# Groups 6 and 7 of a fused transformer block: softmax pieces exponentiated in one ScalarE instruction instead of eight

## The chip, the cores and the metric

The kernel runs on one NeuronCore of a Trainium2 chip. Five instruction queues run side by side: TensorE (PE, with its weight loads as PEld), VectorE (DVE), ScalarE (ACT), GpSimd (POOL) and SyncE (SP). Each takes its instructions strictly in the order in which they are written and waits on semaphores where it needs another engine. The metric is the device time of one execution in microseconds; less is better.

## What is computed

Two batches of 1024 tokens of width 256 pass four layers, each added to its input: a 16-head cross attention on 77 context rows, a feed-forward layer of width 1024 with a layer norm behind it, a single-head cross attention on the same context, and a linear layer whose weights are picked by token position. The change touches the softmax of the first layer:

```python
scores = jnp.einsum('bqhd,bkhd->bhqk', q, k) * scale
weights = jax.nn.softmax(scores, axis=-1)
out = jnp.einsum('bqhk,bkhd->bqhd', weights, v).reshape(B, Lq, D)
```

## The kernel before

The 2048 tokens are cut into 8 groups g of 256. A group has two tiles i of 128 tokens, and the 16 heads fall into two halves a of 8 heads. So a group has four score pieces (g, i, a), each 128 tokens by 8 heads x 77 keys = 616 columns. All groups run through all four layers in a software pipeline: while groups 6 and 7 are in the first layer (about 150 to 200 us of the span), groups 3 to 5 are in the feed-forward and the second attention. The order on each engine is a list written out by hand (the calls at the end of `tensor`, `vector`, `scalar` and `gpsimd`). No scheduler changes it.

The steps of a piece in the first layer, in order:

- `sc` (TensorE, L386): the scores, into one of the two score halves of PSUM, S0 or S1.
- `smax` (VectorE, L666): the negated maximum by head. Where `apart(g, i, a)` holds, `smax` also adds it to the 616 columns (L671), which moves them from PSUM to the tile E in SBUF.
- `ex` (ScalarE): where `apart` holds, one exp over 616 columns of E (L1058). Otherwise eight exps of 77 columns, one a head, straight from PSUM with the maximum as bias and the row sum as a second output (L1067).
- `ssum` (VectorE): where `apart` holds, it first sums E by head (L680); then in both cases the reciprocal (L683).
- `en` (GpSimd, L1261): two multiplications of 308 columns by the reciprocals.
- `tE` (TensorE, L396) transposes E into the same score halves, `et` (ScalarE) copies it out, `pv` (TensorE, L408) multiplies by the values, `o` (ScalarE, L1084) copies the result, `wo` (TensorE, L268) is the output projection, and `x1` (VectorE, L688) adds it to the tokens.

A score half is let go by `sub` (the subtraction) where `apart` holds and by `ex` where it does not. The four banks PB0 to PB3 carry everything else of TensorE; each is let go by the step that reads it, and the next piece in the same bank waits for that.

Names of other steps that stand between these: `lo` (L645) takes the low half of a transposed tile for the split multiplication, and `lo("B", 4)` lets go of PB3, in which `cp(2, 3)` (L455, a transpose of the second attention) comes next. `ql` (L653) is the same for the queries and waits for `qh` on ScalarE. `hl` (L693) is the low half of the hidden layer; it is read by `w2`, and `hl(5, 3)` also lets go of the bank that `w2(5, 0, 0)` takes. `y` (L700) takes the feed-forward's result, `x3_` (L738) that of the second attention. On GpSimd, `bo` (L1254) adds a bias and `rs` (L1215 to L1226) makes the scale and shift of a norm from its statistics. On ScalarE `apply` (L1034) normalises, `hh` (L1090) takes the hidden layer out, and `pc` (L1127) copies tokens for the last layer.

Of the kernel before, what the change touches and what calls it, by code (L numbers as in the profile page):

```python
# [63 lines left out]


def apart(g, i, a):
    return a == 1


def apart_upto(n):  # L70

    return sum(apart(m // 4, m % 4 // 2, m % 2) for m in range(n + 1))


def program(nc, A, out):
    with ExitStack() as ctx:
# [177 lines left out]
        def tensor(e):  # L254
# [119 lines left out]
            def sc(g, i, a, k):  # L374
                b, n = g // 4, 4 * g + 2 * i + a
                w.wait_ge(s["ql"], g + 1)
                w.wait_ge(s["qh"], g + 1)
                w.wait_ge(s["kbl"], b + 1)
                w.wait_ge(s["kba"], 4 * b + 4)
                P = hold(("sc", g, i, a), ("S", k), ("sub", apart_upto(n)) if apart(g, i, a) else ("ex", n + 1))  # L380
                ts = slice(i * 128, (i + 1) * 128)

                for j, (Q, KB) in enumerate(((XTH, KBH), (XTH, KBL), (XTL, KBH))):
                    for u in range(2):
                        own = slice(64 * u, 64 * u + 64)
                        t = e.matmul(P[:, u * 512:u * 512 + 4 * NK], Q[own, 1 + g % 2, a, ts],  # L386
                                     KB[own, b, 4 * a:4 * a + 4, :].rearrange("p h k -> p (h k)"),
                                     start=j == 0, stop=j == 2)
                t.then_inc(s["sc"], 1)
# [175 lines left out]
        def vector(e):  # L565
# [92 lines left out]
            def smax(g, i, a):  # L658

                n = 4 * g + 2 * i + a  # L660
                sv = two(bank("sc", g, i, a))[:, :, 0:4 * NK].rearrange("p u (h k) -> p u h k", k=NK)
                w.wait_ge(s["sc"], n + 1)
                if g:
                    w.wait_ge(s["ex"], n - 3)
                top = two(SX[:, i, 0, 8 * a:8 * a + 8])
                e.tensor_reduce(top, sv, AX, ALU.max, negate=True).then_inc(s["mx"], 1)  # L666
                if apart(g, i, a):
                    w.wait_ge(s["mx"], n + 1)
                    if g:
                        w.wait_ge(s["tE"], n - 3)  # L670
                    e.tensor_tensor(E[:, i, a, 0:8 * NK].rearrange("p (u h k) -> p u h k", u=2, h=4), sv,  # L671
                                    top.unsqueeze(3).to_broadcast([128, 2, 4, NK]), ALU.add).then_inc(s["sub"], 1)
# [782 lines left out]
```

## Time and profile before

| | |
|---|---|
| median of three runs | 271.42 us (271.34 to 272.66) |
| the profiled execution | 271.57 us, of it a span of 269.7 us |
| TensorE busy | 247.4 us, 92% |
| VectorE busy | 218.2 us, 81% |
| GpSimd busy | 189.6 us, 70% |
| ScalarE busy | 160.7 us, 60% |

The rows further below come from this one execution. A timeline row gives the start, the duration, the instruction and, in brackets, how long the engine was idle before it and what ended that. Durations of neighbouring instructions overlap by their pipelines, so what an instruction really costs its engine is the distance from its start to the start of the next. TensorE's matmul ends are modelled; the starts of its weight loads show when a step was let in. A row of the same line with "x2" stands for several instructions in a row.

### The profile page before, as it was taken

Reading aid. Unit: us, or ns where it says so; the run is one execution under the profiler, and the core shown is the slowest. Engines: PE = TensorE matmul, PEld = TensorE weight load, DVE = VectorE, ACT = ScalarE, POOL = GpSimd, SP = SyncE. Lnnn points to the kernel's source line nnn. Section 1 sums busy time; section 2 is a strip of 40 time slices with the busy share of each in tenths; the row PEclk is TensorE's granted clock in tenths of the full one; section 3 lists DMA queues with packets and bytes.
Section 4 is the critical chain, followed back from the end, with each engine's and each line's share of the span. In section 5 each row is a group of like instructions: output and inputs, shape, how many; then the busy total and the mean of one; then the engine's idle time right before and its main releaser. Section 6 shows DMA issues by size and latency. Waiting matters only on the chain.

```text
span 269.7 us, 6211 instructions
## 1 busy us (share of the span) xinstructions
PE 247.4 (92%) x2048; PEld 219.3 (81%) x2048; DVE 218.2 (81%) x573; ACT 160.7 (60%) x510; POOL 189.6 (70%) x361
## 2 busy tenths in 40 slices
PE   0977799899799999999999999999999999979990
PEld 0776577599798978999799789998989999967880
DVE  2799998999999798982999977898588776879551
ACT  2449795885364676797375888457566442465530
POOL 3267789897859797867298687988789655615474
PEclk9995999999999999999999999999999999999998
DMA  6993020010201155010001411221071000000033
GB/s 167 319 319 121 0 79 2 2 39 12 70 0 43 39 166 187 5 21 2 0 2 39 101 39 57 63 80 40 2 218 55 2 0 2 0 1 4 0 156 156
DMA packets 11156, 17.61 MB, mean 65 GB/s; under 512 B 1377, under 2 KB 7509, under 8 KB 11125
## 3 DMA queue, kind: packets, MB, share of 16 engines
q1 hardware_dynamic: 9333, 11.98, 14.2%
q0 software_dynamic: 1792, 5.24, 6.6%
q8 instruction: 16, 0.26, 0.4%
q14 instruction: 15, 0.12, 0.2%
HBM read 14.07 MB, written 3.15 MB: 64 GB/s over the span
## 4 chain that ended last, share of the span: by engine, by line
PE 70%; DVE 13%; POOL 5%; issue 4%; ACT 4%; DMA 2%; SPq 0%; POOLq 0%; DVEq 0%
PE PB L275 33%; PE PB L268 13%; PE PB L472 7%; PE PB L348 5%; PE S L396 5%; PE PB L408 4%; PE S L386 4%; ACT E L1067 2%; DVE SX L666 2%; DMA WKV<-in_w_k 2%; POOL E L1261 1%; DVE SX L680 1%; POOL SM L1218 1%; DVE XTL L645 1%; POOL out_x L1314 1%
## 5 line engine op out<-in xcount | busy, mean ns | idle before, releaser
L1261 POOL TENSOR_TENSOR E<-E,SX 128x308 f32<-128x308 f32 x64 | 43.9, 712 | 10.0 <-DVE SX L683 9.8
L1067 ACT ACTIVATE E<-S,SX 128x77 f32<-128x77 f32 x128 | 39.4, 337 | 10.7 <-DVE SX L666 10.7
L275 PE MATMUL PB<-XTH,W1H 128*128 128x256 f32 x128 | 37.3, 291 | 1.6 <-DVE XTL L645 1.4
L275 PE MATMUL PB<-W2H,HH 128*128 128x256 f32 x128 | 37.5, 293 | 0.0
L275 PE MATMUL PB<-W2H,HL 128*128 128x256 f32 x128 | 35.7, 279 | 0.0
L275 PE MATMUL PB<-W2L,HH 128*128 128x256 f32 x128 | 35.7, 279 | 0.0
L275 PE MATMUL PB<-XTL,W1H 128*128 128x256 f32 x128 | 35.6, 278 | 0.0
L275 PE MATMUL PB<-XTH,W1L 128*128 128x256 f32 x128 | 35.5, 278 | 0.0
L1218 POOL TENSOR_TENSOR SM<-SM,nhalf 128x2 f32<-128x2 f32 x40 | 28.4, 711 | 3.1
L1090 ACT ACTIVATE HH<-PB 128x512 fp32r<-128x512 f32 x32 | 19.1, 600 | 15.9 <-PE PB L275 15.6
L1077 ACT ACTIVATE EW<-S 124x640 f32<-124x640 f32 x32 | 21.9, 711 | 10.8 <-PE S L396 10.7
L1067 ACT ACTIVATION_READ_ACCUMULATOR E<-S,SX 128x1 f32 x128 | 28.0, 219 | 0.0
L275 PEld LDWEIGHTS PB<-XTH,W1H 128*128 128x128 f32 x128 | 24.1, 189 | 2.5 <-DVE XTL L645 1.6
L1215 POOL TENSOR_TENSOR SM<-SM,eps 128x2 f32<-128x2 f32 x32 | 6.7, 210 | 27.3 <-DVE SM L625 27.2
L693 DVE SCALAR_TENSOR_TENSOR HL<-PB,HH 128x512 fp32r<-128x512 f32 x32 | 21.1, 677 | 5.5 <-ACT HH L1090 3.4
L622 DVE BATCH_NORM_STATS2 SM<-X 128x6 f32<-128x256 f32 x64 | 23.7, 413 | 1.6 <-DMA X<-in_x 1.4
L666 DVE TENSOR_REDUCE SX<-S 128x8 f32<-128x616 f32 x32 | 24.5, 785 | 0.7 <-PE S L386 0.7
L275 PEld LDWEIGHTS PB<-W2H,HH 128*128 128x128 f32 x128 | 24.1, 188 | 1.1 <-issue 1.0
L1034 ACT ACTIVATE XN<-X,SM 128x256 f32<-128x256 f32 (+1 forms) x32 | 18.9, 601 | 9.9 <-POOL SM L1224 8.3
L396 PE MATMUL S<-ident,E 128*124 128x128 f32 x160 | 22.1, 274 | 2.6 <-POOL E L1261 1.7
L275 PEld LDWEIGHTS PB<-W2L,HH 128*128 128x128 f32 x128 | 24.2, 189 | 0.1
L275 PEld LDWEIGHTS PB<-W2H,HL 128*128 128x128 f32 x128 | 24.1, 189 | 0.0
(203 smaller groups left out, 727.2 us busy)
## 6 DMA issues: line engine op xcount, KB each, us to landing
RAW<-in_w SPq DMA_DIRECT2D x4, 512.0 KB, 6.0
WD<-in_WD SPq DMA_DIRECT2D x8, 256.0 KB, 3.9
X<-in_x SPq DMA_DIRECT2D x4, 256.0 KB, 5.9
x<-X SPq DMA_DIRECT2D x4, 256.0 KB, 2.2
E<-in_WD SPq DMA_DIRECT2D x4, 256.0 KB
bc<-in_rows SPq DMA_DIRECT2D x1, 640.0 KB, 6.2
X<-in_w1r SPq DMA_DIRECT2D x1, 512.0 KB, 7.9
RT<-in_WD SPq DMA_DIRECT2D x2, 256.0 KB, 2.9
```

The source lines that it names most:

```text
L268: t = e.matmul(dst, a, b, start=j == 0, stop=j == len(pairs) - 1)
L275: t = e.matmul(dst, a, b, start=first and j == 0, stop=last and j == n - 1)
L396: t = e.transpose(P[0:CW, c * 128:(c + 1) * 128], E[:, i, a, c * CW:(c + 1) * CW], ident[:, :])
L622: step(e.bn_stats(smi(K, g, i, 0, 6), src[:, i, :]))
L666: e.tensor_reduce(top, sv, AX, ALU.max, negate=True).then_inc(s["mx"], 1)
L693: e.scalar_tensor_tensor(out=HL[:, hs, :], in0=two(bank("w1", g, j)[:, :]), scalar=0.0, in1=f(HH[:, hs, :]), op0=ALU.max, op1=ALU.subtract ...
L1034: e.activation(dst_of(K, g)[:, 1, 0:n], src_of(K, g)[:, 1, 0:n], ACT.Identity, bias=smi(K, g, 1, 10, 11), scale=smi(K, g, 1, 9, 10)).then_ ...
L1067: t = e.activation(Ei[:, h * NK:(h + 1) * NK], P[:, at:at + NK], ACT.Exp, bias=SX[:, i, 0, k:k + 1], accum_out=SX[:, i, 1, k:k + 1])
L1077: e.activation(ET[:, g % 2, a, :, ts], P[0:CW, 0:640].rearrange("p (c t) -> p c t", c=5), ACT.Copy).then_inc(s["et"], 1)
L1090: e.activation(HH[:, 2 * j:2 * j + 2, :], two(bank("w1", g, j)[:, :]), ACT.Relu).then_inc(s["hh"], 1)
L1218: e.tensor_tensor(sm(K, g, 9), sm(K, g, 8), nhalf[:, :], ALU.pow).then_inc(s["rs" + K], 1)
L1261: t = e.tensor_tensor(Eh, Eh, SX[:, i, 2, 8 * a + h:8 * a + h + 4].unsqueeze(2).to_broadcast([128, 4, NK]), ALU.mult)
```

## The change

`apart` decides for each piece which of the two forms above is used. Before, it held for every piece of the second half, a = 1. Now it holds for all pieces of groups 6 and 7 too, so four pieces change form: (6, 0, 0), (6, 1, 0), (7, 0, 0) and (7, 1, 0). For each of them ScalarE issues one exp instead of eight exps with row sums, and VectorE issues a subtraction and a sum by head that it did not issue before. The score half of such a piece is now let go by the subtraction. Nothing else differs.

```diff
 def apart(g, i, a):
-    return a == 1
+    return a == 1 or g > 5
```

VectorE at the start of group 6, from the application of a norm to `lo("B", 4)`. Before:

```order
264 L639 TENSOR_SCALAR XN<-X,SM 128x256
265 L666 TENSOR_REDUCE SX<-S 128x8 x2
266 L671 TENSOR_TENSOR E<-S,SX 128x616
267 L645 TENSOR_TENSOR XTL<-PB,XTH 128x512
268 L688 TENSOR_TENSOR X<-PB,X 128x2x256
269 L666 TENSOR_REDUCE SX<-S 128x8
270 L645 TENSOR_TENSOR XTL<-PB,XTH 128x512
```

And now:

```order
264 L639 TENSOR_SCALAR XN<-X,SM 128x256
265 L666 TENSOR_REDUCE SX<-S 128x8
266 L671 TENSOR_TENSOR E<-S,SX 128x616
267 L666 TENSOR_REDUCE SX<-S 128x8
268 L671 TENSOR_TENSOR E<-S,SX 128x616
269 L645 TENSOR_TENSOR XTL<-PB,XTH 128x512
270 L688 TENSOR_TENSOR X<-PB,X 128x2x256
271 L666 TENSOR_REDUCE SX<-S 128x8
272 L671 TENSOR_TENSOR E<-S,SX 128x616
273 L645 TENSOR_TENSOR XTL<-PB,XTH 128x512
```

Two subtractions are new ahead of the second L645, which is `lo("B", 4)`.

VectorE in group 7, from the third `hl` of group 5 to the application of a norm. Before:

```order
306 L666 TENSOR_REDUCE SX<-S 128x8
307 L693 SCALAR_TENSOR_TENSOR HL<-PB,HH 128x512
308 L683 RECIPROCAL SX<-SX 128x8
309 L680 TENSOR_REDUCE SX<-E 128x8
310 L683 RECIPROCAL SX<-SX 128x8
311 L639 TENSOR_SCALAR XN<-X,SM 128x256
```

And now:

```order
313 L666 TENSOR_REDUCE SX<-S 128x8
314 L671 TENSOR_TENSOR E<-S,SX 128x616
315 L693 SCALAR_TENSOR_TENSOR HL<-PB,HH 128x512
316 L680 TENSOR_REDUCE SX<-E 128x8
317 L683 RECIPROCAL SX<-SX 128x8
318 L680 TENSOR_REDUCE SX<-E 128x8
319 L683 RECIPROCAL SX<-SX 128x8
320 L639 TENSOR_SCALAR XN<-X,SM 128x256
```

The subtraction of (7, 1, 0) stands ahead of `hl(5, 3)`, the L693 row, and the sum of (7, 0, 0) behind it.

## Rows read from the trace of the kernel before

**Rows 1.** The page's chain that ended last, by engine, share of the span.
```profile
PE 70%; DVE 13%; POOL 5%; issue 4%; ACT 4%; DMA 2%; SPq 0%; POOLq 0%; DVEq 0%
```

**Rows 2.** Busy time by stretch: busy us (instructions) per engine, clock, DMA.
```profile
150.00:200.00 50.00, 50.00 (x460) 44.67 (x453) 40.74 (x102) 33.81 (x114) 40.71 (x72) 1.00 0.25 68
```

**Rows 3.** Waits of TensorE's weight loads, 150 to 200 us: total us, times, longest.
```profile
PEld S L386 <- issue: 0.9, 3, 0.4
...
PEld PB L408 <- ACT EW L1077: 0.3, 1, 0.3
```

**Rows 4.** Groups by line, 150 to 200 us: busy us, mean ns | idle before.
```profile
L1067 ACT ACTIVATE E<-S,SX 128x77 f32<-128x77 f32 x32 | 9.8, 333 | 3.5 <-DVE SX L666 3.5
...
L671 DVE TENSOR_TENSOR E<-S,SX 128x616 f32<-128x616 f32 x4 | 3.2, 800 | 0.1
L680 DVE TENSOR_REDUCE SX<-E 128x8 f32<-128x616 f32 x4 | 3.1, 769 | 0.0
...
L1058 ACT ACTIVATE E<-E 128x616 f32<-128x616 f32 x4 | 2.9, 722 | 0.0
```

**Rows 5.** Timeline, VectorE, piece (6, 1, 1): start us, duration us, instruction [idle before].
```profile
161.87 0.80 DVE L666 TENSOR_REDUCE SX<-S 128x8 f32<-128x616 f32 x1
162.70 0.80 DVE L671 TENSOR_TENSOR E<-S,SX 128x616 f32<-128x616 f32 x1
163.41 0.78 DVE L680 TENSOR_REDUCE SX<-E 128x8 f32<-128x616 f32 x1
164.23 0.20 DVE L683 RECIPROCAL SX<-SX 128x8 f32<-128x8 f32 x1
```

**Rows 6.** Timeline, VectorE, smax(6, 1, 0), lo("B", 4) and ql(7).
```profile
155.92 0.80 DVE L666 TENSOR_REDUCE SX<-S 128x8 f32<-128x616 f32 x1 [0.24 <-PE S L386]
156.63 0.68 DVE L645 TENSOR_TENSOR XTL<-PB,XTH 128x512 fp32r<-128x512 f32 x1
...
158.36 0.88 DVE L653 SCALAR_TENSOR_TENSOR XTL<-PB,cols,XTH 128x256 fp32r<-128x256 f32 x2
```

**Rows 7.** Timeline, weight loads of cp(2), tE(6, 0), w2(5, 0) and wo(7).
```profile
158.00 0.21 PEld L455 LDWEIGHTS PB<-ident,PP 128*77 128x77 f32 x2 [0.18 <-issue]
...
165.61 1.12 PEld L396 LDWEIGHTS S<-ident,E 128*124 128x124 f32 x10
...
184.56 0.19 PEld L275 LDWEIGHTS PB<-W2H,HH 128*128 128x128 f32 x1 [0.41 <-issue]
...
198.30 1.60 PEld L268 LDWEIGHTS PB<-Wo,RT 128*128 128x128 f32 x8
```

**Rows 8.** Timeline, GpSimd: bo(7), en(6, 0, 1), en(7, 1, 1), end of rs("D", 1).
```profile
162.34 1.44 POOL L1254 TENSOR_TENSOR X<-X,bc 128x256 f32<-128x256 f32 x2
164.51 1.36 POOL L1261 TENSOR_TENSOR E<-E,SX 128x308 f32<-128x308 f32 x2 [0.74 <-DVE SX L683]
...
191.70 1.35 POOL L1261 TENSOR_TENSOR E<-E,SX 128x308 f32<-128x308 f32 x2 [0.46 <-DVE SX L683]
...
195.90 0.20 POOL L1224 TENSOR_TENSOR SM<-SM 128x2 f32<-128x2 f32 x1
```

**Rows 9.** Timeline, VectorE: hl(4, 3), y(4), hl(5, 3), x1(6), ssum(7, 1, 1).
```profile
168.61 0.69 DVE L693 SCALAR_TENSOR_TENSOR HL<-PB,HH 128x512 fp32r<-128x512 f32 x1 [1.99 <-issue]
...
175.08 0.69 DVE L700 TENSOR_TENSOR XN<-PB,XN 128x512 f32<-128x512 f32 x1 [0.64 <-PE PB L275]
...
183.39 0.68 DVE L693 SCALAR_TENSOR_TENSOR HL<-PB,HH 128x512 fp32r<-128x512 f32 x1
...
187.96 0.69 DVE L688 TENSOR_TENSOR X<-PB,X 128x512 f32<-128x512 f32 x1 [0.58 <-PE PB L268]
...
191.42 0.20 DVE L683 RECIPROCAL SX<-SX 128x8 f32<-128x8 f32 x1
```

**Rows 10.** Timeline, ScalarE: two applications, then o(7).
```profile
195.86 1.08 ACT L1034 ACTIVATE XN<-X,SM 128x255 f32<-128x255 f32 x2
...
197.46 0.58 ACT L1084 ACTIVATE RT<-PB 128x512 f32<-128x512 f32 x1
```

## The prediction

> **What bounds the kernel now.** I read the page's chain that ended last first: 70% of it is TensorE [rows 1]. Then the busy time of the stretch in which groups 6 and 7 are in the first layer, 150 to 200 us: TensorE is busy 50.00 of 50 us, VectorE 40.7, GpSimd 40.7, ScalarE 33.8 [rows 2]. A busy TensorE is modelled, so I checked the waits of its weight loads in the same stretch. Seven rows, from "S L386 <- issue" with 0.9 us to two of 0.2, add up to 3.1 us, and only one of them names ScalarE: 0.3 us for an `et` [rows 3]. So TensorE sets the pace. Work taken from another engine is worth what TensorE waits for it, nearly nothing here. A step that comes late to TensorE moves everything behind it, since later waits are as short as these. The question is how much slack VectorE has before each step that it feeds.
>
> **What ScalarE gives up.** 32 exps of 77 columns, 9.8 us busy, with as many reads of the row sum, go; four exps of 616 columns at 722 ns come [rows 4]. ScalarE had 16 us free in this stretch already [rows 2], and the 32 exps had waited 3.5 us for VectorE's maxima [rows 4]. I cost this gain at nothing: the one wait of TensorE for ScalarE there [rows 3] is for the `et` of a piece that keeps its form.
>
> **What VectorE takes on.** A piece that has the new form already shows it start to start: maximum to subtraction 0.83 us, subtraction to the next 0.71, sum to reciprocal 0.82 [rows 5]. A maximum without a subtraction lets the next instruction in after 0.71 (155.92 to 156.63) [rows 6]. So the subtraction costs 0.83 + 0.71 - 0.71 = 0.83 us and the sum 0.82. Four pieces: 4 x 1.65 = 6.6 us. VectorE was idle for about 9 us of the 50 [rows 2], but not where it is needed. I follow it past each step that TensorE reads.
>
> Step 1, `lo("B", 4)`. The subtractions of (6, 0, 0) and (6, 1, 0) stand before it: 1.66 us, less the 0.24 that VectorE waited for the scores of (6, 1, 0) [rows 6], gives 1.4. Its row ends at 156.63 + 0.68 = 157.3 [rows 6], so now at 158.7. `cp(2, 3)` needs its bank, and its weight load started at 158.00 [rows 7]. With 0.05 us for the semaphore it starts at 158.75. **TensorE +0.75.** (The scores of (6, 1, 0) wait for a later subtraction too, about 0.2 us; that is inside this.) `ql(7)`, which TensorE needs next, loses 1.2 and not 1.4, because it had waited for ScalarE; it ends at 158.36 + 0.88 + 1.2 = 160.4 [rows 6], just when the moved TensorE wants its bank.
>
> Step 2, `en(6, 0, 1)`. Behind `ql(7)` comes the new sum of (6, 0, 0), so the reciprocal that GpSimd waits for is 1.2 + 0.8 = 2.0 us later, and `bo(7)` behind it too: from 162.34 to 164.3, over at 165.8. `en(6, 0, 1)` therefore starts at 165.8 and not at 164.51, and ends at 167.15 [rows 8]. TensorE's ten transposes started at 165.61 and last 1.12 [rows 7]; the second five, which need this piece, began near 166.15, with the shift 166.9. **TensorE +0.25, in all 1.0.**
>
> Between: `hl(4, 3)` had waited 1.99 us [rows 9], for ScalarE by the order of the work, and that swallows VectorE's lag. From there the sum of (6, 1, 0) is already behind and one more subtraction, (7, 0, 0), is ahead of `y(4)`, where VectorE waited 0.64 for TensorE [rows 9]. I get VectorE 1.1 late at `y(4)`, level with TensorE's 1.0.
>
> Step 3, `hl(5, 3)`. One subtraction more, (7, 1, 0): 1.1 + 0.83 = 1.9 late, ending at 183.39 + 0.68 + 1.9 = 186.0 [rows 9]. `w2(5, 0, 0)` started at 184.56 [rows 7]. **TensorE now 1.5 late.**
>
> Step 4, GpSimd and ScalarE ahead of `wo(7)`. The sums of (7, 0, 0) and (7, 1, 0) put the reciprocal of (7, 1, 1) 1.9 + 2 x 0.82 = 3.5 us back, less 0.58 that VectorE waited before `x1(6)` [rows 9]: 2.9. Its row is 191.42 [rows 9], so now 194.3, and `en(7, 1, 1)` follows 0.28 behind as before (191.70) [rows 8], at 194.6. From there GpSimd's queue runs without a gap to the end of `rs("D", 1)`, 195.90 + 0.20 - 191.70 = 4.4 us [rows 8]: 199.0. ScalarE's second application waits for that, and behind it `pc(0)` and then `o(7)`. Three such works took 197.46 - 195.86 = 1.6 us before [rows 10], two take 1.1: `o(7)` starts at 200.1 and ends at 200.7. `wo(7)` started at 198.30 [rows 7] and now can't before 200.75. **TensorE 2.45 late, the sum.** The 0.2 us that TensorE may stop for (7, 1, 0) on the way is inside it.
>
> VectorE then waits for TensorE at `y(5)`, which takes up its own lag, and behind 200 us everything waits for TensorE as before. The sum stands against the profiled execution: 271.57 + 2.4 = 274.0. That execution is 0.15 above the median of the runs, so the forecast is 271.4 + 2.4, **273.9 us**.
>
> What no row prices: whether more work of VectorE beside GpSimd slows either. `bo(7)` took 1.44 us [rows 8] with a subtraction and a sum beside it [rows 5], and the same amount elsewhere, so I take nothing; at the worst 0.1 us for each of the four. Below, each step has its error: the idle times used are of 0.2 to 0.6 us, and an error of 0.3 in one can undo steps 2 or 3, not 1 and 4 together.
>
> **The rivals.**
>
> A, most of it hidden. Step 1 holds and the lag of GpSimd and ScalarE in step 4 does not reach TensorE, for instance because the 0.46 us that GpSimd waited before `en(7, 1, 1)` [rows 8] and ScalarE's time off shorten its chain. Then 271.4 + 0.75, up to 1.3: 272.2 to 272.7. For it: the four steps are margins of a few tenths. Against: step 4 is a sum of 2.9 us of lag over a margin of 0.26 (`o(7)` over at 198.04, read at 198.30) [rows 7, 10].
>
> B, TensorE has slack that its rows hide, and nothing moves: 271.4. The weight loads are busy only 44.7 of the 50 us [rows 2], and the 5.3 left would cover 2.4. The waits say otherwise: 3.1 us, in pieces of at most 0.4 [rows 3], each of which comes again. The Trainium skill, "Perfetto Trace Analysis", section "Identifying the Most-Contended Engine", says that headroom of TensorE is to be judged by the weight loads' busy share and not by matmul busy time. By that rule B would hold and the time would be 271.4; the trace only bears out the difference between the two (44.7 and 50.0), not that a late step is made up.
>
> C, faster. The mechanism: in the old form S0 is let go by the last of eight exps, and now by the subtraction, which is sooner, and ScalarE reaches `hh` and `et` earlier, so that TensorE's waits of 0.9 us before the scores and 0.3 before `pv` [rows 3] go, with a few of the rest. At most 1.5: 269.9. It decides if VectorE's lag never passes 0.7 us at `cp(2, 3)`, the slack there (157.3 to 158.00) [rows 6, 7]. But the two subtractions alone are 1.66.
>
> D, worse: as forecast, and GpSimd slower beside VectorE, or `ql(7)` and (7, 1, 0) stop TensorE on their own account. 275.5.
>
> **How the numbers follow.** Forecast (1.4 to 3.5 slower) 0.62; A 0.19; B 0.09; C 0.05; D 0.05. A measurement of this kernel tells 0.5% from no change, 1.36 us, so the border is 272.8. Slower: 0.62 + 0.05 = 0.67. Same: A and B, 0.28. Faster: C, 0.05. The range runs from 271.5 (leaving out B and C, 0.14) to 275.4 (half of D).
>
> **What would show it.** In the changed kernel: `cp(2, 3)` starts 0.7 to 0.8 later than at 158.00, with a wait for L645; the second half of the transposes of group 6 comes after `en` on GpSimd; `w2(5, 0, 0)` waits for L693; and before `wo(7)` TensorE waits more than 0.5 us for L1084. TensorE's waits in 150 to 202 us rise from 3.1 to over 5. I am wrong if these waits are absent, or if they are there and the span does not grow by their sum.

## The result

The changed kernel takes 274.93 us, median of four runs (273.63 to 276.8), against 271.95 for the kernel before in the same session: a ratio of 1.0116, interval 1.0068 to 1.0164. A second session gave 274.78 against 272.16, ratio 1.0088 (1.0056 to 1.0120). So it is slower by about 1%, 2.4 to 3.2 us by the two ratios; the forecast was 273.9. The ratios leave out runs over 1.5% above the fastest of the same kernel; one such run of the kernel before took 412.58 us, at a mean granted clock of 0.565.

The profiled execution took 273.63 us, of it a span of 271.8. That is 2.1 over the profiled execution of before, but the two did not start alike: TensorE's first weight load started at 5.63 us and not at 6.52, and TensorE reached the scores of (6, 0, 0), ahead of which nothing is changed, at 150.33 us and not at 151.34.

Timeline, weight loads, first load of the scores of (6, 0, 0), of the kernel before:

```profile
151.34 0.19 PEld L386 LDWEIGHTS S<-KBH,XTH 64*128 64x128 f32 x2 [0.41 <-issue]
```

and of the changed kernel:

```profile
150.33 0.19 PEld L386 LDWEIGHTS S<-KBH,XTH 64*128 64x128 f32 x2 [0.41 <-issue]
```

Counted from this load, the changed kernel loses 2.86 us by `wo(7)` and 3.1 by the end. All "late" figures below are counted from it.

**Profile after.** The page's chain that ended last, by engine, which answers to [rows 1]:

```profile
PE 56%; DVE 23%; issue 7%; POOL 7%; ACT 4%; DMA 1%; POOLq 0%; SPq 0%; DVEq 0%; ACTq 0%
```

TensorE's share of the chain fell from 70% to 56%, VectorE's rose from 13% to 23%. Busy time of 150 to 200 us (span piece, PE, PEld, DVE, ACT, POOL, clock, DMA, GB/s), which answers to [rows 2]:

```profile
150.00:200.00 50.00, 48.05 (x432) 42.78 (x424) 44.54 (x101) 25.92 (x52) 38.36 (x69) 1.00 0.21 59
```

VectorE is busy 3.8 us more in these 50 us, ScalarE 7.9 less. (The four subtractions and four sums are 6.3 us of busy time; part of VectorE's other work has moved out of the stretch, since everything in it comes later.) The groups by line, 150 to 202.3 us, answer to [rows 4]: the exps of 77 columns are gone, and the three rows of 616 columns now count eight instructions each.

```profile
L671 DVE TENSOR_TENSOR E<-S,SX 128x616 f32<-128x616 f32 x8 | 6.4, 800 | 0.3
L680 DVE TENSOR_REDUCE SX<-E 128x8 f32<-128x616 f32 x8 | 6.2, 776 | 0.0
L1058 ACT ACTIVATE E<-E 128x616 f32<-128x616 f32 x8 | 5.6, 712 | 7.8 <-DVE E L671 7.8
```

ScalarE now waits 7.8 us for subtractions: the time that it saves is spent waiting. Waits of the weight loads, 150 to 202.3 us (total us, times, longest), which answers to [rows 3]:

```profile
PEld PB L275 <- issue: 1.1, 2, 1.0
PEld PB L268 <- ACT RT L1084: 0.8, 1, 0.8
PEld S L386 <- issue: 0.7, 2, 0.4
PEld PB L455 <- issue: 0.7, 1, 0.7
PEld S L396 <- POOL E L1261: 0.6, 1, 0.6
```

With six smaller rows they add up to 5.7 us, against 3.1 before. Four of the five rows are new or longer. Here these four are in the timeline, `cp(2)`, `w2(5, 0)`, `tE(7, 1)` and `wo(7)`, which answers to [rows 7]:

```profile
157.76 0.21 PEld L455 LDWEIGHTS PB<-ident,PP 128*77 128x77 f32 x2 [0.73 <-issue]
...
185.03 0.19 PEld L275 LDWEIGHTS PB<-W2H,HH 128*128 128x128 f32 x1 [0.97 <-issue]
193.55 0.52 PEld L396 LDWEIGHTS S<-ident,E 128*124 128x124 f32 x5 [0.58 <-POOL E L1261]
...
200.15 0.94 PEld L268 LDWEIGHTS PB<-Wo,RT 128*128 128x128 f32 x5 [0.76 <-ACT RT L1084]
```

"issue" names no releaser. VectorE's rows do, just ahead of the first two loads: `lo("B", 4)` ends at 157.64, `hl(5, 3)` at 184.92. The same rows show `apply("D", 0)` (L639) and the reciprocal of (7, 1, 1), and answer to [rows 6, 9]:

```profile
156.96 0.68 DVE L645 TENSOR_TENSOR XTL<-PB,XTH 128x512 fp32r<-128x512 f32 x1
...
184.24 0.68 DVE L693 SCALAR_TENSOR_TENSOR HL<-PB,HH 128x512 fp32r<-128x512 f32 x1
...
186.68 0.76 DVE L639 TENSOR_SCALAR XN<-X,SM 128x256 f32<-128x256 f32 x1
...
193.67 0.20 DVE L683 RECIPROCAL SX<-SX 128x8 f32<-128x8 f32 x1
195.73 0.69 DVE L700 TENSOR_TENSOR XN<-PB,XN 128x512 f32<-128x512 f32 x1 [1.86 <-PE PB L275]
```

GpSimd, `bo(7)`, `en(6, 0, 1)`, the four multiplications beside `apply("D", 0)`, then `en(7, 1, 1)` and the end of `rs("D", 1)`, which answers to [rows 8]:

```profile
163.28 1.44 POOL L1254 TENSOR_TENSOR X<-X,bc 128x256 f32<-128x256 f32 x2
164.68 1.36 POOL L1261 TENSOR_TENSOR E<-E,SX 128x308 f32<-128x308 f32 x2
...
186.50 2.81 POOL L1261 TENSOR_TENSOR E<-E,SX 128x308 f32<-128x308 f32 x4
...
193.95 1.36 POOL L1261 TENSOR_TENSOR E<-E,SX 128x308 f32<-128x308 f32 x2 [0.46 <-DVE SX L683]
...
198.17 0.21 POOL L1224 TENSOR_TENSOR SM<-SM 128x2 f32<-128x2 f32 x1
```

ScalarE, the second application, `pc(0)` and `o(7)`, which answers to [rows 10]:

```profile
198.41 0.60 ACT L1034 ACTIVATE XN<-X,SM 128x256 f32<-128x256 f32 x1 [0.94 <-POOL SM L1224]
198.91 0.71 ACT L1127 ACTIVATE XP<-XTE 128x256 f32 x2
199.53 0.57 ACT L1084 ACTIVATE RT<-PB 128x512 f32<-128x512 f32 x1
```

From 193.67 to 200.15 one thing hangs on the other without a gap: reciprocal, multiplications, scale and shift of the norm, application, `pc(0)`, `o(7)`, `wo(7)`.

### The profile page after: what moved, and what is told of

It reads as the page before. It is cut to its first block, busy times and chain, and to the rows that moved or that the text cites. A ratio compares the mean times of both kernels' runs of the same rounds, so it can differ in the third digit from the quotient of the medians.

```text
span 271.8 us, 6162 instructions
## 1 busy us (share of the span) xinstructions
PE 248.2 (91%) x2048; PEld 219.9 (81%) x2048; DVE 224.9 (83%) x581; ACT 154.0 (57%) x450; POOL 190.1 (70%) x361
## 4 chain that ended last, share of the span: by engine, by line
PE 56%; DVE 23%; issue 7%; POOL 7%; ACT 4%; DMA 1%; POOLq 0%; SPq 0%; DVEq 0%; ACTq 0%
PE PB L275 27%; PE PB L268 10%; PE PB L472 7%; DVE SX L666 4%; PE PB L348 3%; PE S L386 3%; PE S L396 3%; DVE SX L680 3%; PE PB L408 2%; POOL E L1261 2%; ACT E L1067 2%; DVE SM L622 2%; POOL SM L1218 2%; DVE XN L639 2%; DVE XTL L645 1%
## 5 line engine op out<-in xcount | busy, mean ns | idle before, releaser
L1067 ACT ACTIVATE E<-S,SX 128x77 f32<-128x77 f32 x96 | 29.6, 339 | 7.2 <-DVE SX L666 7.2
L693 DVE SCALAR_TENSOR_TENSOR HL<-PB,HH 128x512 fp32r<-128x512 f32 x32 | 21.1, 677 | 4.6 <-ACT HH L1090 4.6
L275 PEld LDWEIGHTS PB<-XTL,W1H 128*128 128x128 f32 x128 | 24.1, 189 | 0.1
```

The costliest lines, as they stand in the source:

```text
L275: t = e.matmul(dst, a, b, start=first and j == 0, stop=last and j == n - 1)
L693: e.scalar_tensor_tensor(out=HL[:, hs, :], in0=two(bank("w1", g, j)[:, :]), scalar=0.0, in1=f(HH[:, hs, :]), op0=ALU.max, op1=ALU.subtract ...
L1067: t = e.activation(Ei[:, h * NK:(h + 1) * NK], P[:, at:at + NK], ACT.Exp, bias=SX[:, i, 0, k:k + 1], accum_out=SX[:, i, 1, k:k + 1])
```

## The experiments

One table for all of them: how many us later than in the kernel before TensorE starts each step, counted from the scores of (6, 0, 0). `e10` repeats the kernel before in this stretch and shows how exact the measure is: 0.01. `tE(6, 0)` is read at the first of its ten transposes. The end is less exact: it comes from spans given to 0.1 us, `after_again` and `e1` lose 2.7 and 3.0 us between 240 and 250 us (last section), and `e3`, `e6` and `e7` lose 0.9 to 1.0 in the last 8 us, from a cause that stays open. Apart from that each kernel's lag behind `wo(7)` still stands, to 0.2 us, when its last 8 us begin.

| kernel | cp(2) | tE(6, 0) | w2(5, 0) | tE(7, 1, 0) | behind wo(7) | end |
|---|---|---|---|---|---|---|
| after | 0.77 | 0.97 | 1.48 | 2.11 | 2.86 | 3.11 |
| after_again | 0.76 | 0.96 | 1.48 | 2.10 | 2.86 | 5.73 |
| e1_group6 | 0.76 | 0.76 | 0.82 | 0.82 | 0.83 | 3.92 |
| e2_group7 | 0.01 | 0.02 | 0.57 | 1.20 | 1.95 | 2.20 |
| e3_sub_only | 0.76 | 0.97 | 1.48 | 1.49 | 1.49 | 2.46 |
| e4_act_full | 0.76 | 0.77 | 1.39 | 3.72 | 4.47 | 4.59 |
| e5_lo_first | 0.20 | 0.72 | 1.39 | 3.72 | 4.47 | 4.53 |
| e6_o_first | 0.76 | 0.77 | 1.44 | 3.77 | 4.37 | 5.21 |
| e7_three_old | 0.00 | 3.23 | 3.22 | 4.45 | 4.43 | 5.38 |
| e8_apply_early | 0.77 | 0.78 | 1.41 | 1.90 | 2.66 | 2.69 |
| e9_all_moves | 0.17 | 0.71 | 0.83 | 2.07 | 2.66 | 2.65 |
| e10_group0_old | -0.01 | 0.00 | 0.00 | 0.00 | 0.00 | 0.06 |

**The change once more, and halved.** `after_again` is the changed kernel unchanged; the other two take one group each.

> The changed kernel once more, beside the kernel before on the same chip, to separate the change from what an execution's start adds. All lags here are counted from the weight load of the scores of (6, 0, 0), since the two profiled executions already differ by 1.0 us there, before anything changed. Theory: the lag of TensorE is 0.8 us at cp(2, 3), 1.5 at w2(5, 0, 0), 2.9 at wo(7) and 3.1 at the end, as in the first profile of the changed kernel, and the ratio of the medians is 1.011. Rival: part of the 3.1 us came from that one execution; then the lags come out different by more than 0.3 us.

```diff
-    return a == 1 or g > 5
+    return a == 1 or g == 6
```

> Only group 6 has all pieces in the new form (two changed pieces instead of four). Theory (steps late at TensorE one after the other): lag 0.8 us at cp(2, 3), 0.8 to 1.0 at pv(6), and no more after it: end 1.0 late, about 272.5 if before is 271.5. Rival (only the last step counts, and the first is given back later): end 0 to 0.3 late.

```diff
-    return a == 1 or g > 5
+    return a == 1 or g == 7
```

> Only group 7 has all pieces in the new form. Theory: nothing at cp(2, 3); w2(5, 0, 0) about 0.6 late; wo(7) waits for o(7) and is 2.0 to 2.4 late, end the same, about 273.7 if before is 271.5. With the 1.0 of group 6 this makes up the 3.1. Rival (each half is hidden alone and only both together are too much): end under 1.0 late.

`after_again` falls on `after` to 0.01 us in all columns but the last. Group 6 alone gave 273.32 (271.93 to 275.29; ratio 1.0053, 1.0021 to 1.0085), group 7 alone 275.19 (274.21 to 278.11; 1.0147, 1.0084 to 1.0210). By the trace group 6 costs 0.83 us, 0.76 of it at `cp(2)` and the rest inside `tE(6, 0)`; group 7 costs 0.57 at `w2(5, 0)`, 0.6 at `tE(7, 1, 0)` and 0.75 at `wo(7)`. 0.83 + 1.95 is 2.78 of the whole change's 2.86: nothing later makes up more than 0.1 us of a delay of TensorE, and the two groups hardly meet. Only at `w2(5, 0)` does 0.57 grow to 0.66 behind group 6's lag.

**Subtractions without sums.** VectorE subtracts, ScalarE does the eight exps with row sums, now from E.

```diff
-                if apart(g, i, a):
+                if a:
...
-                    t = e.activation(Ei, Ei, ACT.Exp)
+                    if a:
+                        t = e.activation(Ei, Ei, ACT.Exp)
+                    else:
+                        for h in range(8):
+                            t = e.activation(Ei[:, h * NK:(h + 1) * NK], Ei[:, h * NK:(h + 1) * NK], ACT.Exp,
+                                             accum_out=SX[:, i, 1, h:h + 1])
```

> The four pieces are subtracted by VectorE as in the changed kernel, but ScalarE then issues eight exps with row sums that read E, so VectorE does not sum. This separates the subtraction (0.83 us each) from the sum (0.82 each) and gives ScalarE its old work back. Theory (VectorE's added instructions are the price): lag 0.8 us at cp(2, 3) as in the changed kernel, 1.5 at w2(5, 0, 0) as there since only subtractions stand before it, and at wo(7) 1.6 us less than in the changed kernel, hidden behind the 1.5: end 1.5 to 1.8 late. Rival (ScalarE's saved time hid part of the price): end 3 late or more.

275.88 us (272.0 to 276.83), too scattered for a ratio; its trace is as clear as the others. Up to `w2(5, 0)` it equals the changed kernel, and then it loses nothing more: 1.49 at `wo(7)`. Weight loads of `tB(6)`, the transposes ahead of the feed-forward, and behind them `cs(4)`, the scores of the second attention, and `wo(7)` without a new stop (the 0.41 was there before the change):

```profile
199.95 0.42 PEld L348 LDWEIGHTS PB<-ident,XN 128*128 128x128 f32 x4 [0.41 <-DVE XN L639]
200.33 0.97 PEld L268 LDWEIGHTS PB<-M,XN 128*128 128x128 f32 x8
201.22 1.60 PEld L268 LDWEIGHTS PB<-Wo,RT 128*128 128x128 f32 x8
```

So the subtractions make 1.5 us (steps 1 and 3) and the sums, with what they push back, the other 1.4 (step 4).

**Is ScalarE's saving worth anything?** All of VectorE's new work, and ScalarE keeps the eight exps too.

```diff
-                    t = e.activation(Ei, Ei, ACT.Exp)
+                    if a:
+                        t = e.activation(Ei, Ei, ACT.Exp)
+                    else:
+                        for h in range(8):
+                            t = e.activation(Ei[:, h * NK:(h + 1) * NK], Ei[:, h * NK:(h + 1) * NK], ACT.Exp,
+                                             accum_out=SX[:, i, 0, h:h + 1])
```

> VectorE does all of the changed kernel's work (subtraction and sum for four more pieces), and ScalarE still issues eight exps with row sums for these pieces, reading E; its row sums are not used. This takes ScalarE's saving away from the changed kernel and leaves the rest. Theory (ScalarE's saving is worth nothing, and its longer exp delays the sums only where they follow closely): same lags as the changed kernel at cp(2, 3), 0.8, and w2(5, 0, 0), 1.5; at wo(7) 2.9, at most 0.5 more where a sum now waits for the longer exp. Rival (the saving hid part of the price): over 3.5 at wo(7).

277.19 us (275.19 and 279.19; ratio 1.0198, 0.9995 to 1.0402). The lags up to `w2(5, 0)` are no larger than the change's, even 0.1 to 0.2 smaller (by the spacing of matmuls, last section): ScalarE's saving is worth nothing there. Then the kernel stands at 3.72 instead of 2.11, and the cause is one VectorE instruction, `apply("D", 0)`, and GpSimd beside it:

```profile
186.62 2.63 DVE L639 TENSOR_SCALAR XN<-X,SM 128x256 f32<-128x256 f32 x1
189.17 0.79 DVE L666 TENSOR_REDUCE SX<-S 128x8 f32<-128x616 f32 x1
```

```profile
186.41 2.67 POOL L1266 TENSOR_TENSOR E<-E,SX 128x308 f32<-128x308 f32 x4
```

The same instruction took 0.76 in the changed kernel and lets its successor in after 0.69. In the kernel before it lies at 185.00, takes 0.37, and is over before GpSimd begins its four multiplications at 186.47.

Timeline of the kernel before, VectorE and then GpSimd:

```profile
185.00 0.37 DVE L639 TENSOR_SCALAR XN<-X,SM 128x256 f32<-128x256 f32 x1
```

```profile
186.47 2.77 POOL L1261 TENSOR_TENSOR E<-E,SX 128x308 f32<-128x308 f32 x4
```

The 2.63 also stood in `e5` and `e6`, whose VectorE work up to there is that of the changed kernel (in `e6` in the same order too); these three ran on one chip in one session. 0.76 stood in `after`, `after_again` and `e2`. What decides is open (last section). The sign that the expectation gave for the rival, over 3.5 at `wo(7)`, is there, but it is not the saving: `e5` and `e6` have the saving and the same stall, and they are 4.47 and 4.37 late behind `wo(7)`, where `e4` without the saving is 4.47. By an estimate, taking off the longer stall (2.55 - 0.69 = 1.9 from start to start), `e4` would be near 2.6 late there, no more than the changed kernel.

**Moving steps forward in the changed kernel.** `e5` puts `lo("B", 4)` ahead of the maximum of (6, 1, 0); `e6` puts `o(7)` ahead of the second application.

```diff
-            apply("B", 4); ...; lo("A", 7); x1(5); smax(6, 1, 0)
-            lo("B", 4); stats("B", 5); ql(7); ssum(6, 0, 0)
+            apply("B", 4); ...; lo("A", 7); x1(5); lo("B", 4)
+            smax(6, 1, 0); stats("B", 5); ql(7); ssum(6, 0, 0)
```

> The changed kernel, with lo("B", 4) on VectorE one place earlier, ahead of smax(6, 1, 0) with its new subtraction. This takes the cause of step 1 away and nothing else. Theory: cp(2, 3) no longer waits (lag under 0.2 instead of 0.8), and since VectorE waits for ScalarE at hl(4, 3) and for nothing else after it, all later lags shrink by the same: w2(5, 0, 0) 0.7 to 0.9, wo(7) 2.1 to 2.3, end 2.3 instead of 3.1. Rival (the later stops are set by VectorE's total work and not by what came before): lag small at cp(2, 3) but back at 1.5 by w2(5, 0, 0) and 2.9 at wo(7).

```diff
-            et(7, 1, 1); apply("B", 6); apply("D", 1); pc(0); o(7); hi("B", 6)
+            et(7, 1, 1); apply("B", 6); o(7); apply("D", 1); pc(0); hi("B", 6)
```

> The changed kernel, with o(7) on ScalarE ahead of apply("D", 1) and pc(0). This takes away the queueing of step 4: o(7) no longer stands behind work that waits for GpSimd. Theory: lags as in the changed kernel up to w2(5, 0, 0), 1.5, and to the second transposes of group 7, 2.0; wo(7) then adds nothing: 2.0 instead of 2.9, end 2.2. Rival (x2(5) and lo("B", 6), which wait for rs("Y", 5) in the same GpSimd queue, stop w1(6) anyway): lag back at 2.8 by w1(6).

`e5`: 276.3 us (276.22 and 276.38). The stop at `cp(2)` is gone, 0.20 instead of 0.77, but 2.2 us later TensorE stops 0.41 us for `ql(7)`, which still stands behind the same subtractions, and then 0.18 inside `tE(6, 0)` for `en(6, 0, 1)`. From `tE(6, 0)` on the lag is that of `e4` and `e6`, to 0.1 us. Timeline of `e5`, weight loads and then GpSimd's `en(6, 0, 1)`:

```profile
158.37 0.21 PEld L455 LDWEIGHTS PB<-ident,PP 128*77 128x77 f32 x2 [0.18 <-issue]
...
160.58 0.19 PEld L275 LDWEIGHTS PB<-XTH,W1H 128*128 128x128 f32 x1 [0.41 <-DVE XTL L653]
...
167.26 0.52 PEld L396 LDWEIGHTS S<-ident,E 128*124 128x124 f32 x5 [0.18 <-POOL E L1261]
```

```profile
165.85 1.36 POOL L1261 TENSOR_TENSOR E<-E,SX 128x308 f32<-128x308 f32 x2
```

The expectation that the lags behind would shrink with the first one fell. `e6`: 277.01 us (275.75 and 278.26). No stop before `wo(7)`, but one of 0.69 before the next transposes, `tD(1)`, which need the application that `o(7)` has passed. The wait changed its name.

```profile
203.28 0.42 PEld L348 LDWEIGHTS PB<-ident,XN 128*128 128x128 f32 x4 [0.69 <-issue]
```

**What the new form buys.** Here three pieces of the second half, (6, 1, 1), (7, 0, 1) and (7, 1, 1), have the old form, and all others are as in the kernel before.

```diff
-    return a == 1 or g > 5
+    return a == 1 and 2 * g + i < 13
```

> The opposite of the change, from the kernel before: pieces (6, 1, 1), (7, 0, 1) and (7, 1, 1) go to the old form too, so VectorE has about 5 us less to do and ScalarE about 5.4 more. Theory (TensorE never waited for VectorE long in this stretch): nothing is gained, lag between -0.3 and 0.3 at every step. Rival (TensorE's pace is set by VectorE or ScalarE there): a gain of over 0.5, or ScalarE becomes late and it loses over 0.5.

278.09 us (277.95 and 278.24; ratio 1.0232, 1.0126 to 1.0337), the slowest, where no change was expected. TensorE stops 3.2 us before `tE(6, 0)`: its score half is now let go only by the exps of (6, 1, 1), and on ScalarE those stand behind `cpt(3)`, while the subtraction stands on VectorE and is done at once. Before `tE(7, 1, 0)` it stops 1.3 us more. So the new form is worth 3.2 us there, where an early release of a score half is what TensorE needs. In the kernel before, TensorE did not wait for the release of any of the four pieces of the change: what follows each in its score half is `sc(6, 1, 1)`, the second transposes of `tE(6, 0)`, the first of `tE(6, 1)` and `tE(7, 0)`, and none of these shows a wait.

**Taking `apply("D", 0)` out of GpSimd's way**, and then all moves together.

```diff
-            smax(7, 1, 0); hl(5, 3); ssum(7, 0, 0); ssum(7, 0, 1); apply("D", 0); smax(7, 1, 1); apply("C", 4); x1(6)
+            smax(7, 1, 0); hl(5, 3); apply("D", 0); ssum(7, 0, 0); ssum(7, 0, 1); smax(7, 1, 1); apply("C", 4); x1(6)
```

> The changed kernel, with apply("D", 0) on VectorE ahead of ssum(7, 0, 0) instead of behind ssum(7, 0, 1). It then runs while GpSimd issues transfers and not beside the four multiplications of en(7, 0, 0) and en(7, 0, 1), where its one instruction took 0.76 us in two profiles and 2.63 in three, against 0.37 in the kernel before. Nothing else changes. Theory (the two engines block each other there): it takes under 0.5 us; the second transposes of group 7 are 1.7 late (not 2.1 or 3.7), wo(7) 2.4 late (not 2.9 or 4.5), and the executions of the kernel scatter less. Rival (VectorE's instruction was late for another reason, a wait inside it): still 0.76 or 2.63 in the new place, lags as before.

```diff
-            ...; x1(5); smax(6, 1, 0)
-            lo("B", 4); stats("B", 5); ql(7); ...
+            ...; x1(5); lo("B", 4)
+            smax(6, 1, 0); ql(7); stats("B", 5); ...
...
-            smax(7, 1, 0); hl(5, 3); ssum(7, 0, 0); ssum(7, 0, 1); apply("D", 0); smax(7, 1, 1); ...
+            hl(5, 3); apply("D", 0); smax(7, 1, 0); ssum(7, 0, 0); ssum(7, 0, 1); smax(7, 1, 1); ...
...
-            ...; apply("B", 6); apply("D", 1); pc(0); o(7); hi("B", 6)
+            ...; apply("B", 6); o(7); apply("D", 1); pc(0); hi("B", 6)
```

> The changed kernel, with all four stops taken away by order alone: lo("B", 4) ahead of smax(6, 1, 0), ql(7) ahead of stats("B", 5), hl(5, 3) and apply("D", 0) ahead of smax(7, 1, 0), and o(7) ahead of apply("D", 1) on ScalarE. Theory (the price of the change is where VectorE's added work stands, not how much it is): lag under 0.3 at cp(2, 3), 0.3 to 0.8 at w2(5, 0, 0), 1.0 to 1.8 at wo(7), where the reciprocals of group 7 are still late; the end the same. Rival (VectorE's total work sets the end): 2 or more late at wo(7) all the same.

`e8`: 275.53 us (274.06 to 275.7; ratio 1.0124, 1.0046 to 1.0201). The application at its new place, before GpSimd's multiplications, takes 0.48 instead of 0.76, and `tE(7, 1, 0)` is 1.90 late instead of 2.11 (0.07 of this was there at `w2(5, 0)`). The expected 1.7 there and 2.4 at `wo(7)` were not reached; behind `wo(7)` it is 2.66 late:

```profile
185.58 0.48 DVE L639 TENSOR_SCALAR XN<-X,SM 128x256 f32<-128x256 f32 x1
```

`e9`: 275.03 us (274.21 to 276.12; ratio 1.0117, 1.0026 to 1.0207). It is only 0.83 late at `w2(5, 0)`, and 2.07 at `tE(7, 1, 0)`, where one wait has it all:

```profile
194.57 0.52 PEld L396 LDWEIGHTS S<-ident,E 128*124 128x124 f32 x5 [1.21 <-POOL E L1261]
```

That is the rival on record for `e9`, 2 or more late at `wo(7)` in spite of all moves. VectorE has no idle time between its wait of 0.34 for ScalarE at 184.09 and the last sum at 193.90, so the order inside shifts a delay between TensorE's steps but does not remove it. Three orders of the same work (`after`, `e8`, `e9`) are 2.66 to 2.86 late behind `wo(7)`.

**Another group, and another place.** `e10` undoes the change and gives the second half of group 0 the old form; `e11` is the kernel before with `lo("B", 1)`, a sum and `ql(3)` moved forward into the twenty small steps of `r_pairs`, which stand ahead of them.

```diff
-    return a == 1 or g > 5
+    return a == 1 and g > 0
```

> From the kernel before: the two pieces of group 0 with a = 1 go to the old form, eight exps and no subtraction or sum on VectorE; groups 6 and 7 as before the change. In 18 to 32 us VectorE is on the chain and TensorE waits for it (2.8 us for a subtraction at 21.9 us), the reverse of 150 to 200 us. It takes 3.3 us from VectorE there and gives ScalarE about 3.6 more. Theory (work is worth moving off the engine that the path runs through): 0.5 to 2 us faster than before, about 270.5. Rival (the score half, which is then let go by the last of eight exps and not by the subtraction, stops the next scores and ScalarE becomes the chain): 0 to 3 us slower.

```diff
+                lo("B", 1)
                 step(e.tensor_tensor(big, big, in0(V[:, 0, :], 16), ALU.mult))
...
+                ssum(2, 1, 1)
                 for a, (r, m) in enumerate(((0, 128.0), (1, 512.0), (1, 128.0))):
...
                 e.tensor_copy(EV[:, :, :], B[0:1, 0:3, :]).then_inc(s["route2"], 1)
+                ql(3)
...
-            hl(0, 3); apply("B", 1); lo("A", 3); r_pairs(); lo("B", 1); ssum(2, 1, 1); ql(3); y(0); stats("A", 4)
+            hl(0, 3); apply("B", 1); lo("A", 3); r_pairs(); y(0); stats("A", 4)
```

> The kernel before, without the change under study. Twenty small steps of VectorE from 65.4 to 72.7 us of its trace (L876 to L912) stand ahead of lo("B", 1) at 72.73, for which TensorE waits 1.64 us at 73.46 although the high half had been ready since 67.1. Here lo("B", 1) goes behind the fourth of these steps (67.4 us), the sum of (2, 1, 1) behind the mask (about 70.2) and ql(3), whose ScalarE part is over at 71.9, behind the first cast; the work of VectorE is the same. Theory of this study, a step that comes late to TensorE is paid in full and one that comes early is won: TensorE's wait of 1.64 us falls to under 0.5, its next wait, 0.23 for ql(3), goes or stays, and everything behind 78 us starts 1.0 to 1.8 us earlier; the median is 0.9 to 1.8 us under that of the kernel before. Rival 1: the wait only changes its name, since ScalarE's et at 71.8 to 73.1 and its multiplication by the values, or ql(3), stop TensorE a few hundred ns later: under 0.4 us gained. Rival 2: the route's results come 1.6 to 2.3 us later, and the transfers and GpSimd's work behind them stop something later on: gained at 78 us and lost again by the end.

`e10`: 277.43 us (275.74 to 279.89; ratio 1.0222, 1.0118 to 1.0326). It comes to the scores of (6, 0, 0) at 155.48, 4.1 us later than the kernel before, and equals it from there on; the gain of 0.5 to 2 us that was expected did not come. Counted from the first scores it takes 140.2 us to that point, where the kernels with the same code up to there take 135.2 to 136.5: in group 0 the new form of the second half is worth 3.6 to 5.0 us. TensorE stands 7.0 us for the exps of (0, 0, 1), where it stood 2.9 for their subtraction, and its granted clock is 0.50 from 25 to 30 us and 0.85 from 30 to 35, where it was 0.90 and 1.00 in the kernel before; so part of this price is the clock. Waits of the weight loads of `e10`, 10 to 45 us:

```profile
PEld S L386 <- ACT E L1067: 7.0, 1, 7.0
```

`e11`: 274.22 us (271.4 to 275.5, 11 runs), ratio 1.0047 (1.0006 to 1.0088): no gain, slightly slower. Waits of the weight loads, 60 to 82 us, of `e11`:

```profile
PEld S L386 <- DVE XTL L653: 1.5, 1, 1.5
PEld S L396 <- issue: 1.1, 1, 1.1
```

TensorE no longer stops for `lo("B", 1)`, but 1.5 us for `ql(3)`, and 1.1 more before the transposes of (2, 1, 0), whose score half is let go by the subtraction of (3, 0, 1), and that stands behind the same list. Counted from TensorE's `w2` ahead of it (66.19 before, 67.16 here), it gains 0.5 us and then stands 0.7 behind. VectorE needed 0.7 us more for the same list. In it, it waited 0.30 for ScalarE ahead of `lo("B", 1)`, and its small steps had come to lie otherwise beside GpSimd's work: three took 0.61 to 0.76 instead of 0.17 to 0.25, a fourth 0.64 instead of 0.20, while others got shorter. One of the three:

```profile
70.68 0.76 DVE L897 SCALAR_TENSOR_TENSOR WD<-WD 128x15 f32<-128x15 f32 x1
```

Its median is 2.1 us above the kernel before. TensorE's mean granted clock was 0.972 to 0.975 in eight of its eleven runs, against 0.971 to 0.975 in six of sixteen of the kernel before; how much of the 2.1 us is the clock (last section) was not separated.

No version among these beats the kernel before.

## Why the prediction was right

**What bounds the kernel.** Right: TensorE set the pace, and no delay was made up. Rival B, slack that the weight loads' busy share hides, fell: with 44.7 us busy of 50 [rows 2] not even 0.1 us was recovered (`e1` is 0.82 to 0.83 late from `w2(5, 0)` to `wo(7)`). The Trainium skill, "Perfetto Trace Analysis", section "Identifying the Most-Contended Engine", judges TensorE's headroom by its share of the matmul peak and by the weight loads' busy share. That share does not decide here: it says how full the engine is, and the question was whether a late step is made up.

**Step 1**, +0.75: measured 0.77. `lo("B", 4)` was 1.34 late (forecast 1.4), `ql(7)` 1.1 (1.2). No row of the prediction shows its 0.05 us for the semaphore; the load came 0.12 us behind the end of `lo("B", 4)` here and 0.11 behind `hl(5, 3)`.

**Step 2**, +0.25 by waiting for `en(6, 0, 1)`, 1.0 in all: measured 0.97, but in the changed kernel by another cause. GpSimd was late as forecast (`bo(7)` by 1.95, forecast 2.0), and `en(6, 0, 1)` ended at 166.04. The sixth of the ten transposes from 165.57, the first that needs it, started at 166.11 without a wait. The 0.2 came from the `w1` matmuls before, spaced 0.118 us instead of 0.114 (last section). Where they kept 0.114 the forecast wait is there, but not at the first transpose, where the table reads: in `e1`, `e4`, `e6` and `e8` the first is 0.76 to 0.78 late, the sixth starts 0.05 to 0.06 us behind the end of `en(6, 0, 1)`, and the step behind the ten is 0.88 late. In `e5` and `e9`, where `cp(2)` is only 0.2 late, the same wait brings that step to the same 0.88. So the mechanism was right and worth 0.12 us instead of 0.25, and that the sum came out at 0.97 is in part luck. It also is why moving `lo("B", 4)` alone wins nothing.

**Step 3**, 1.5 in all: measured 1.48. `hl(5, 3)` was 1.86 late (1.9).

**Step 4**, 2.45 in all: measured 2.86. Each link was there in the order foretold. Mis-sized was its first term, the lag of the reciprocal of (7, 1, 1): 3.26 instead of 2.9 us. The missing 0.4 is `apply("D", 0)`, which VectorE reached 0.8 later by the first new sum and so beside GpSimd's multiplications: 0.69 us to its successor and not 0.27. The sentence "what no row prices: whether more work of VectorE beside GpSimd slows either. ... I take nothing" had the wrong reason behind it. A subtraction and a sum beside GpSimd cost nothing, as said; an instruction of another kind that is pushed there by them does. From the reciprocal on, GpSimd took 4.4 us and ScalarE 1.7, as forecast. On the way TensorE stopped 0.58 us at `tE(7, 1, 0)`, where the forecast had 0.2; that is inside the sum as well.

**ScalarE's saving** at nothing: right (`e4`). The waits rose to 5.7 us ("over 5").

**Between the sum and the time.** From `wo(7)` to the end another 0.2 us was lost, 0.15 of it in the next `w1` matmuls, again at 0.118 us. The time is 1.0 over the forecast: 0.5 because the change cost 3.0 us by the medians and not 2.45, and 0.5 because the kernel before had a median of 271.95 in the session of the comparison and not 271.42. (271.4 + 2.4 is 273.8; the 273.9 comes from 271.42 + 2.45.)

**The other rivals.** A fell: the chain of step 4 reached TensorE, which stopped 0.76 us for `o(7)`. C fell by its own condition, VectorE's lag under 0.7 us at `cp(2)`: it was 1.34. D had GpSimd slowed by VectorE; what was measured is one VectorE instruction held up beside GpSimd, by 0.4 us in the changed kernel. In `e4` to `e6`, where it was held 1.9 us longer, the lag behind `wo(7)` is 4.4 to 4.5, close to D's 4.1.

## What to carry to other kernels

Where the bounding engine waits only in small pieces, follow the lag of the engine that takes on work from one step that the bounding engine reads to the next: the largest lag minus the margin there is the price, and it is paid once and in full. An engine that is 19% idle on the whole can have none of it where the change puts the work, and then another order of the same work moves the delay but, in the three orders tried here, does not win it back. And see what a late instruction will newly lie beside, not only what comes later.

## What the runs showed of the hardware

**VectorE beside GpSimd: blocked for one instruction or for four.** The same application of 256 columns took 0.37 us ahead of GpSimd's multiplications in the kernel before, and 0.76 or 2.63 when it was issued 0.2 us behind the first of four. Their row of four started at 186.50 and took 2.81, about 0.70 each: the first was over near 187.20, and the application ended at 187.44. In `e4` all four ended at 189.08 and the application at 189.25. So it seems to have waited for the end of one GpSimd instruction, or of all four. Three executions show either length, and two things go with it, so neither is shown to be the cause: the chip (the three of 2.63 ran on one, in one session), and the moment of issue, 0.18 us behind the first multiplication in the three of 0.76 and 0.20 to 0.21 in the three of 2.63. The Trainium skill, "SBUF — State Buffer", section "Who interferes with whom", says that a VectorE instruction in a mode that uses both of its port pairs, which a `tensor_scalar` can be, shares one pair with GpSimd; whichever issues first holds it for its whole instruction and the other is blocked. The two lengths agree with such a turn; no run here shows which mode the application ran in, and that a waiting instruction can be passed over three times the page does not say. Maxima, sums and subtractions kept 0.75 to 0.80 us beside the same multiplications.

Multiplications are not the only thing that goes with a long application. In `e3` it was issued before them, beside a transfer that GpSimd issues itself, and took 0.90:

```profile
188.29 0.90 DVE L639 TENSOR_SCALAR XN<-X,SM 128x256 f32<-128x256 f32 x1
```

```profile
187.98 0.95 POOL L1298 DMA_INDIRECT X<-x,SI  x1 [0.30 <-issue]
```

Beside the same kind of transfer it took 0.48 in `e8` and 0.37 in the kernel before; what differs is open.

**Two spacings of the same matmuls.** Runs of matmuls of 256 columns come at 0.114 or at 0.118 us from start to start at the same granted clock of 1.00, in kernels with the same code there; 48 of them differ by 0.2 us. What chooses is open.

**TensorE's granted clock behind a thin stretch.** In `after_again` and `e1` (mean 0.66 from 240 to 250 us) and in `e11` (0.83) the clock fell behind 240 us; in the other kernels of the table it stayed at 1.00. Busy time by stretch of `after_again`:

```profile
235.00:240.00 5.00, 3.84 (x20) 3.10 (x19) 4.40 (x12) 1.75 (x6) 2.61 (x6) 1.00 0.00 0
240.00:250.00 10.00, 9.76 (x38) 7.98 (x39) 5.90 (x18) 5.08 (x18) 2.59 (x6) 0.66 0.00 1
```

and of `after`:

```profile
235.00:240.00 5.00, 3.96 (x21) 3.19 (x19) 4.40 (x12) 1.75 (x6) 2.73 (x6) 1.00 0.00 0
240.00:250.00 10.00, 9.61 (x51) 7.74 (x52) 8.20 (x24) 6.19 (x21) 2.61 (x6) 1.00 0.00 1
```

The same program had been busy 3.8 and 4.0 us of the 5 before, waiting 1.5 us for a VectorE chain; in one execution the clock then stayed at 2.4 GHz, in the other it was at 1.2 GHz for part of the stretch, and that one lost 2.7 us by the end. Executions of the kernel before have it too: four of its timed runs, 273.79 to 275.16, show a mean clock of 0.970 or 0.971, and most others 270.5 to 272.9 at 0.975 to 0.986. This is part of the scatter in the medians above, and it is why the steps were read from the lags and not from the times. Whether the change makes such executions more frequent is open.
